# Queries and keys of the later batches computed during the first scan and kept in DRAM (a two-layer gated cross-attention kernel on one core)

## The reference, cut to what matters

```python
# a Mamba-like mixer on the context, gated by silu of the normalised x
x = einsum('bld,ed->bel', ctx, in_proj_w); x = silu(causal_conv4(x) + conv_b)
x_dbl = x_proj(x); dt = softplus(dt_proj(x_dbl[:16]) + dt_b)
state = state * exp(dt * A) + (dt * u) * b ; y = (state * c).sum(n)     # a scan over 512 positions, 16 states
...
# after that a quantised feed-forward block, then attention whose weights come from the context alone
query = einsum('bnc,dc->bnd', ctx, Wq) + bq
key   = einsum('bnc,dc->bnd', ctx, Wk) + bk
energy = einsum('bnd,bmd->bnm', query, key); attention = softmax(energy)
x_m = einsum('bln,bmn->blm', x_normed, attention)
# and a feed-forward block in fp32 with gelu (512 -> 2048 -> 512)
```

## Time and profile before

| | us |
|---|---|
| median of 3 runs | 938.27 (938.05 to 938.3) |
| the profiled execution | 938.1 |
| its span, first to last instruction | 936.3 |

### The profile page before, as it was taken

One profiled execution on the slowest core, in us unless ns is written; L12 is line 12 of the kernel. 1 busy time (PEld: TensorE's weight loads), 2 busy tenths in 40 slices (PEclk: granted clock), 3 DMA queues, 4 the chain that ended last, 5 costly groups with the idle time before them and its releaser, 6 DMA issues. The chain is left out here.

```text
span 936.3 us, 9661 instructions
## 1 busy us (share of the span) xinstructions
PE 850.3 (91%) x2940; PEld 422.0 (45%) x2940; DVE 734.7 (78%) x866; ACT 651.9 (70%) x977; POOL 538.8 (58%) x477
## 2 busy tenths in 40 slices
PE   6586796889999999899999999999999999898999
PEld 2132333444444444444444444444444444457887
DVE  4897899884799998965999998946999998853333
ACT  3887998874888973756889863847889855524442
POOL 4698778122898984314999882227998861032000
PEclk9798997899999999999999999999999999999999
DMA  8389994300299975311599972402899961101321
GB/s 294 94 176 211 237 220 90 135 1 29 68 191 231 241 162 158 107 51 45 124 226 224 241 150 69 158 1 67 182 229 219 201 158 53 60 1 48 110 91 68
DMA packets 50676, 126.93 MB, mean 136 GB/s; under 512 B 6064, under 2 KB 7216, under 8 KB 50112
## 3 DMA queue, kind: packets, MB, share of 16 engines
q0 software_dynamic: 16128, 58.73, 33.6%
q1 hardware_dynamic: 34496, 67.58, 21.1%
HBM read 60.23 MB, written 7.34 MB: 72 GB/s over the span
## 5 line engine op out<-in xcount | busy, mean ns | idle before, releaser
L1867 POOL TENSOR_TENSOR work<-du,bcast 128x1024 f32<-128x1024 f32 x128 | 352.4, 2786 | 9.8 <-ACT bcast L1002 9.7
L1466 DVE TENSOR_TENSOR_SCAN pair<-pair,work 128x512 f32<-128x512 f32 x256 | 299.3, 1215 | 20.0 <-ACT pair L1017 19.6
L1017 ACT ACTIVATE pair<-dt,a_neg 128x512 f32<-128x512 f32 x256 | 166.3, 685 | 26.4 <-DVE work L1473 26.2
L770 PE MATMUL bank<-stage,ring 128*128 128x512 f32 x384 | 172.9, 593 | 1.8 <-ACT stage L1289 1.8
L1473 DVE TENSOR_TENSOR work<-pair,ccast 128x1024 f32<-128x1024 f32 x128 | 156.8, 1225 | 12.0 <-issue 0.5
L1882 POOL DMA_DIRECT2D u<-work x112 | 122.3, 1092 | 35.8 <-DMA u<-work 19.1
L770 PEld LDWEIGHTS bank<-stage,ring 128*128 128x128 f32 x384 | 72.3, 190 | 82.6 <-issue 76.3
L1853 POOL TENSOR_SCALAR fst<-fst 128x1 f32<-128x1 f32 x32 | 14.8, 461 | 139.5 <-DVE fst L1710 139.4
L784 PE MATMUL bank<-ring,stage 128*128 128x512 f32 x192 | 85.6, 594 | 1.7 <-ACT hx L1332 1.7
L651 PE MATMUL pair<-w1q,qT 128*128 128x512 bf16 x256 | 59.1, 379 | 9.2 <-ACT qT L1267 6.9
L515 PE MATMUL bank<-xd,pick 128*128 128x512 bf16 x128 | 50.2, 392 | 16.8 <-ACT bcast L1002 10.5
(11 more groups left out here) (186 smaller groups left out, 1527.5 us busy)
## 6 DMA issues: line engine op xcount, KB each, us to landing
u<-work POOLq DMA_DIRECT2D x112, 512.0 KB, 5.9
ring<-ffn_dram SPq DMA_DIRECT2D x120, 256.0 KB, 5.0
ring<-ffn_dram SPq DMA_DIRECT2D x16, 512.0 KB, 3.3
xres<-x_dram SPq DMA_DIRECT2D x4, 1024.0 KB, 5.3
stage<-w_dram SPq DMA_DIRECT2D x1, 4096.0 KB, 17.1
stage<-w_dram SPq DMA_DIRECT2D x4, 1024.0 KB, 7.6
out_dram<-stage SPq DMA_DIRECT2D x16, 256.0 KB, 2.1
ahead_dram<-hT SPq DMA_DIRECT2D x12, 256.0 KB, 3.8
```

Of the source, the lines that this page charges most:

```text
L770: last = pe.matmul(banks[UP_BANKS[f % 3]][:], piece(b, f)[:, k * P:(k + 1) * P], xnT[:, k, :], start=k == 0, stop=k == J - 1)
L1017: act.activation(pairs[s % DECAYBUFS][:, q, :], dt[:, p * HALF + q, :], ACT.Exp, scale=a_neg[:, p * HALF + q, n:n + 1]).then_inc(s_decay, 1)
L1466: dve.tensor_tensor_scan(pair[:, q, :], pair[:, q, :], rows[:, q, :], 0.0, ALU.mult, ALU.add).then_inc(s_scan, 1)
L1867: pool.tensor_tensor(work[:, s % SCANBUFS, :, :], du[:, p * HALF:(p + 1) * HALF, :], bcast[:, n % 2, :].unsqueeze(1).broadcast_to([P, HALF ...
```

## The change

`query` and `key` of batches 1 to 3 are no longer made in the later passes. A new DRAM buffer `qk_dram` holds them. In the first scan, behind `ahead_project(a)` for the second and the third part of each batch (a = 1, 2, 5, 6, 9, 10), TensorE makes one of the two products into bank 3 (`ahead_qk`, 4 records), ScalarE copies it to two free rows of `ring` (`ahead_qk_copy`) and SyncE stores it (`store_qk`, 256 KB each). The product waits for `s_aout`, that is for ScalarE's `ahead_out(a - 1)`, which empties bank 3 in the same half; the convolution of part a, in the next half, waits for the copy. In each later pass SyncE loads the pair into `qk` (`load_qk`, 512 KB) behind the load of `u`; `qk_products`, `qk_copy` and the waits on them are gone from the later passes, and so are the two `load_context` of passes 1 and 2. Batch 0 keeps its own.

```diff
+    qk_d = nc.dram_tensor("qk_dram", (B - 1, 2, P, L), F32, kind="Internal").ap()
+        qk_rows = ring[:, J:J + 2, :]
@@ SyncE
+                    for i in range(2):
+                        sp.wait_ge(s_qkstored[i], len(AHEAD_BATCHES) * 16)
...
+            def store_qk(g, i):
+                sp.wait_ge(s_aqk, 2 * g + i + 1)
+                sp.dma_start(qk_d[AHEAD_BATCHES[g] - 1, i], qk_rows[:, i, :]).then_inc(s_qkstored[i], 16)
+
+            def load_qk(b):
+                sp.wait_ge(s_y, b * 2)
+                if b == 1:
+                    for i in range(2):
+                        sp.wait_ge(s_qkstored[i], len(AHEAD_BATCHES) * 16)
+                sp.dma_start(qk, qk_d[b - 1].rearrange("i p l -> p i l")).then_inc(s_qkload, 16)
...
                     load_u(b + 1)
+                    load_qk(b + 1)
...
-                    if context_after:
-                        load_context(b + 2)
...
+            def store_group(g, a):
+                store_ahead(g * J + a)
+                if a < 2:
+                    store_qk(g, a)
@@ TensorE
                 pe.wait_ge(s_arows, a + 1)
                 if a:
                     pe.wait_ge(s_aout, a)
-                else:
+                if a % J in (1, 2):
+                    pe.wait_ge(s_aqk, a // J * 2 + a % J)
...
+            def ahead_qk(g, i):
+                pe.wait_ge(s_aout, g * J + i + 1)
+                rows = ctxT if AHEAD_BATCHES[g] == 1 else ctx_spare
+                for k in range(KC):
+                    last = pe.matmul(banks[3][:], wqk[:, k, i, :], rows[:, k, :], start=k == 0, stop=k == KC - 1)
+                last.then_inc(s_aqkmm, 1)
...
                 a = ahead_at(slot, which, p, 0)
                 if a is not None:
                     ahead_project(a)
+                    if a % J in (1, 2):
+                        ahead_qk(a // J, a % J - 1)
...
                 else:
-                    pe.wait_ge(s_qk, b * 2 + 2)
-                    if prev is not None:
-                        pe.wait_ge(s_fgelu, prev * FT + FT)
+                    pe.wait_ge(s_qkload, b * 16)
+                    pe.wait_ge(s_fgelu, prev * FT + FT)
...
-                elif f == 2:
-                    pe.wait_ge(s_qk, (b + 1) * 2 + 2)
...
-                    if slot == QK_SLOT:
-                        qk_products(m, prev, 0)
+                    if slot == QK_SLOT and not rest:
+                        qk_products(0)
...
-                    if slot == (QK_SLOT + 1 if rest else QK_SLOT):
-                        qk_products(m, prev, 1)
+                    if slot == QK_SLOT and not rest:
+                        qk_products(1)
@@ ScalarE
+            def ahead_qk_copy(g, i):
+                act.wait_ge(s_aqkmm, 2 * g + i + 1)
+                if g:
+                    act.wait_ge(s_qkstored[i], g * 16)
+                act.activation(qk_rows[:, i, :], banks[3][:], ACT.Identity, bias=bqk[:, i:i + 1]).then_inc(s_aqk, 1)
...
                 a = ahead_at(slot, which, p, 0)
                 if a is not None:
                     ahead_copy(a)
+                    if a % J in (1, 2):
+                        ahead_qk_copy(a // J, a % J - 1)
...
                         if rest:
                             norm_copy(b, 5)
-                        qk_copy(m, prev, 0)
+                        else:
+                            qk_copy(0)
```

More of the change, by code:

```diff
@@ L283, in program @@
         s_uload = sem("s_uload")
+        s_aqkmm = sem("s_aqkmm")
+        s_aqk = sem("s_aqk")
+        s_qkstored = [sem(f"s_qkstored{i}") for i in range(2)]
+        s_qkload = sem("s_qkload")
         s_inproj = sem("s_inproj")
@@ L450, in load_context, with run @@
             def load_context(b):
-                sp.wait_ge(s_qkmm, (b - 1) * 2 + 2)
+                sp.wait_ge(s_qkmm, 2)
                 sp.dma_start(ctxT[:], ctxT_d[b].rearrange("(k p) l -> p k l", p=P)).then_inc(s_ctx, 16)
-            def run(b, more, context_after):
+            def store_qk(g, i):
[7 more added lines that the diff above has]
+                sp.dma_start(qk, qk_d[b - 1].rearrange("i p l -> p i l")).then_inc(s_qkload, 16)
+            def run(b, more):
                 if more:
                     load_u(b + 1)
+                    load_qk(b + 1)
                     for k in range(PIECES):
@@ L482, in _ @@
             load_context(1)
-            store_ahead(0)
-            store_ahead(1)
-            store_ahead(2)
+            def store_group(g, a):
+                store_ahead(g * J + a)
+                if a < 2:
+                    store_qk(g, a)
+            store_group(0, 0)
+            store_group(0, 1)
+            store_group(0, 2)
             load_spare(2)
-            store_ahead(3)
+            store_group(0, 3)
             load_second(0)
-            store_ahead(4)
-            store_ahead(5)
+            store_group(1, 0)
+            store_group(1, 1)
             load_second(1)
-            store_ahead(6)
+            store_group(1, 2)
             load_second(2)
-            store_ahead(7)
+            store_group(1, 3)
             load_second(3)
-            for a in range(2 * J, AHEADS):
-                store_ahead(a)
+            for a in range(J):
+                store_group(2, a)
             for i in range(0, B - 2):
-                run(i, True, True)
-            run(B - 2, True, False)
-            run(B - 1, False, False)
+                run(i, True)
+            run(B - 2, True)
+            run(B - 1, False)
             sp.wait_ge(s_out, B * T * 16)
@@ L562, in ahead_convolve @@
                     pe.wait_ge(s_aout, a)
-                else:
+                if a % J in (1, 2):
+                    pe.wait_ge(s_aqk, a // J * 2 + a % J)
+                if a == 0:
                     pe.wait_ge(s_taps, J * TAPS)
@@ L599, in step_sizes, with qk_products @@
                               start=True, stop=True).then_inc(s_dtmm, 1)
-            def qk_products(b, prev, i):
+            def qk_products(i):
                 if i:
-                    pe.wait_ge(s_qk, b * 2 + 1)
+                    pe.wait_ge(s_qk, 1)
                 else:
-                    pe.wait_ge(s_ctx, b * 16 + 16)
+                    pe.wait_ge(s_ctx, 16)
                 for k in range(KC):
@@ L612, in energies @@
                     pe.wait_ge(s_att, b * J + j)
-                else:
-                    pe.wait_ge(s_qk, b * 2 + 2)
-                    if prev is not None:
-                        pe.wait_ge(s_fgelu, prev * FT + FT)
+                elif prev is None:
+                    pe.wait_ge(s_qk, 2)
+                else:
+                    pe.wait_ge(s_qkload, b * 16)
+                    pe.wait_ge(s_fgelu, prev * FT + FT)
                 pe.matmul(banks[1][:], qk[:, 0, j * P:(j + 1) * P], qk[:, 1, :],
@@ L763, in f_up @@
                     pe.wait_ge(s_fgelu, b * FT + f - 2)
-                elif f == 2:
-                    pe.wait_ge(s_qk, (b + 1) * 2 + 2)
-                else:
+                elif f < 2:
                     pe.wait_ge(s_xnTc, b * 2 * T + 2 * T)
@@ L944, in pass_ @@
                         norm_transpose(b, 7)
-                        pe.wait_ge(s_qk, m * 2 + 1)
                         keep_awake(6, 1)
@@ L1205, in att_copy, with qk_copy @@
                                ACT.Copy, bias=-1.0 / D).then_inc(s_att, 1)
-            def qk_copy(b, prev, i):
-                act.wait_ge(s_qkmm, b * 2 + i + 1)
+            def qk_copy(i):
+                act.wait_ge(s_qkmm, i + 1)
                 act.activation(qk[:, i, :], banks[1][:], ACT.Identity, bias=bqk[:, i:i + 1]).then_inc(s_qk, 1)
@@ L1366, in pass_ @@
                         ahead(slot, 0, 1)
-                    if slot == (QK_SLOT + 1 if rest else QK_SLOT):
-                        qk_copy(m, prev, 1)
+                    if slot == QK_SLOT and not rest:
+                        qk_copy(1)
                     if slot == QK_SLOT and rest:
```

## The result

The changed kernel takes **950.03 us** (median of 4 runs, 948.52 to 950.97) beside 938.28 for the kernel before (4 runs, 938.05 to 938.88): ratio 1.0123, 95% interval 1.0105 to 1.014. It is 11.8 us slower. Forecast were 948.4 us and a range of 942.0 to 951.5. The profiled execution took 948.52 us, the fastest of the four, and its span is 946.7.

The account below looks back on a forecast made before the run. Bounds: in the first scan, ScalarE and TensorE handing work over every half; in later scans, GpSimd at half 6. Profiled 938.1 + 10.9 (first scan) - 0.6 (later passes) = 948.4 us; range 942.0 to 951.5.

Parts of the forecast that it names:

- 2.19 us a product in the first scan: First scan: each of six products delays ScalarE 2.19 us, 0.58 of it work and 1.6 standing beside TensorE.
- 2.2 us hidden in parts 1 and 2: First scan: of 4.4 us ScalarE lateness, 2.2 is taken up at its wait for the weights' mean.
- 4.4 us each from parts 5 and 6 and from parts 9 and 10: First scan: behind each of these pairs of parts, the full 4.4 us delay goes through.
- The sum, 10.3 us: Whole kernel: 10.9 us lost in the first scan less 0.6 gained in later passes, 10.3 us slower.
- the distance from scan to scan: Later scans, a sign to check in the profile: distance between scans stays the same within 0.5 us.
- The clock term at 83.59: First scan's convolution at 83.59: nothing booked; TensorE idles some 3.6 us; full clock would return at most 1.8 us.
- rival D: First scan: hidden 2.2 us come through, or TensorE falls to half clock in new waits; 950.6 to 953 us, chance 0.10.
- 0.2 us a later pass: Later passes: removing the products gains 0.2 us each, 0.6 in all, as GpSimd sets the time at half 6.
- ScalarE's longer wait for GpSimd: Later scans, half 6, a sign to check: ScalarE's 0.31 us wait for GpSimd's input remains and grows longer.
- rival B: Later passes: the wait for GpSimd gives way and 2.1 us a pass are kept; 942.6 us, chance 0.12.
- C: Later scans: TensorE is the bound, 10.3 us come off, first scan pays at most the copies; 931.3 us, chance 0.06.
- Stores at zero: SyncE's added stores cost nothing: each takes 3.8 us, and only loads used tens of us later wait behind them.

Follow-up runs that it names:

- e3: Changed kernel with the six products in another bank and earlier halves, not waiting for ScalarE's pair, copied at the end of the next half: 939.97 us, ratio 1.0015.
- e8: Kernel before plus the first scan's added products, copies and stores for parts 1 and 2 alone: 943.06 us, ratio 1.005.
- e2: Kernel before plus the first scan's six products, copies and stores; later passes as before: 950.52 us, ratio 1.0116.
- e7: As e2, but without the six products; copies, the convolution's wait and stores stay: 943.75 us, ratio 1.0061.
- e4: Changed kernel with GpSimd's bias steps of blocks 2 and 3 moved from slot 5 to slots 8 and 9: 941.8 us, ratio 1.0035 to the kernel before.
- e1: Changed kernel without the first scan's products; batch 0's queries and keys are stored instead and loaded by later passes: 942.88 us, ratio 1.0041.
- e11: As e1, but with neither stores nor loads of queries and keys; batches 1 to 3 use batch 0's in place: 938.83 us, ratio 0.9989.

## Why the forecast held, and where it did not

- **2.19 us a product in the first scan:** measured 2.29, of the same make-up (product, copy, two hops). The idle times in front of the six copies show this standing directly, and in e3, which has neither it nor the products so late, VectorE's scan is 1.61 - 0.32 = 1.3 us longer than before, not 11.6.
- **2.2 us hidden in parts 1 and 2:** VectorE is 2.5 us late behind them (half 9, less the start), forecast 2.2; e8 gives 2.7.
- **4.4 us each from parts 5 and 6 and from parts 9 and 10:** 7.16 - 2.58 = 4.6, and 11.73 - 7.16 = 4.6. So the scan is 11.6 us longer instead of 10.9.
- **The sum, 10.3 us against 10.4 in the profiled executions (948.52 - 938.1), is nearer than its terms, and that is luck.** The scan cost 0.7 us more than booked and started 0.1 later, and the later scans gave 0.7. But from the first scan to the second it is 82.69 us instead of 84.76, 2.1 less: TensorE's fillers took 6.70 us instead of 7.39 (granted clock 0.78 against 0.61 in the four microseconds where they begin), and a stretch at half clock at 224 to 228 us (0.62) is in the kernel before alone. And from the second scan to the third it is 83.31 us instead of 81.63, for the changed kernel has the stretch of 434 to 440 us shown above and the kernel before has none in the like place (1.00 at 424 to 430 us). Nobody booked these two; they nearly cancel. The second is also why the distance from scan to scan, said to be the same within 0.5 us, grew from 200.32 to 201.77 once; the other fell from 201.98 to 201.56.
- **The clock term at 83.59:** TensorE idled 3.63 us there, forecast 3.6, and came out at half clock all the same (5.4 us in all), as booked. A fall of the clock behind the wait in front of a convolution, as in rival D, happened in e2, e7 and e8 and not in the profiled run of the changed kernel, whose waits there were no shorter than e2's.
- **0.2 us a later pass:** 0.23, and ScalarE's longer wait for GpSimd stands where the forecast had it. TensorE's idle time grew too, 0.58 us in front of the broadcast (forecast 0.9) and 0.67 in front of the unit before it. Rivals B and C, by which 2.1 to 3.4 us a pass come off, are out for the change as made. e4 shows what rival B needed: not TensorE early, but GpSimd.
- **Stores at zero: wrong.** The forecast looked at who waits behind them on SyncE. It did not ask what their traffic does to GpSimd's accumulating DMAs, nor how near GpSimd's last small steps lie to VectorE's gating. By e1 against e11 that is 0.5%, some 4 to 5 us, part of it TensorE's clock behind the waits. In the changed kernel it stays hidden, since VectorE is later than GpSimd: the four steps end at 171.24 and the gating begins at 173.60. In e3, where the scan is cheap, the last step meets the gating and ScalarE waits 3.34 us; there the term counts.
- **The parts don't add:** e2's 1.2% and e1's 0.4% against 1.2% for the whole. That the hidden steps are the reason follows from the changed kernel's trace; no run tests it by itself.

The Trainium skill (Perfetto Trace Analysis, Identifying the Most-Contended Engine) would have the engine of highest occupancy optimized first, in the first scan VectorE. That work on a less busy engine would fit beneath it the runs don't bear out: six copies on ScalarE, which had idle time, made the scan 11.6 us longer with the waits around them. In the later scans 10.3 us taken from TensorE, the busiest by the rows at 97%, gave 0.7; the page itself does not judge TensorE by its busy share.

## What to carry to other kernels

When two in-order engines hand work to each other in every half, price an added step by where it stands in the handshake, not by its duration: put the product where its input is long ready and the copy a stage later. Before expecting a gain from an engine at 97%, look for a second chain that ends at the same wait, and move both. Price a new transfer by the DMAs of other queues that it meets as well, and by what those hold up next.

## What the hardware showed unexpectedly

- One-column steps of GpSimd take 0.24 to 0.56 us alone and 0.60 to 1.38 us under VectorE's gating in e1; one took 2.10 us in e3. In the kernel before they are over 0.01 us ahead of it.
- The convolution of part 7 took 3.70 us at full clock after 2.50 us of idling in the kernel before (at 108.87) and after 2.43 in the changed kernel (116.03), but 5.23 after 2.49 in e8 (112.96) and 5.40 after 2.43 in e2 (116.35). The idle time just before it doesn't alone tell whether the clock falls.
- Single runs of one kernel spread by 2 to 8 us (e3: 936.03 to 944.47), and a run's mean granted clock goes with it: of the kernel before, runs at 0.978 took 934.7 to 935.4 us and runs at 0.969 to 0.971 took 940.5 to 941.6.
